# A hybrid attention block on one core: the hyperbolic stage as one stream of 32 heads, with ScalarE on four chunks per instruction

## What is computed

```python
q_h, k_h, v_h = exp_map(x @ W_q.T), exp_map(x @ W_k.T), exp_map(x @ W_v.T)    # per head, 16 wide
arg    = max(1 + 2*c*|q - k|^2 / max((1 - c|q|^2) * (1 - c|k|^2), EPS), 1 + EPS)
dist   = arccosh(arg) / sqrt(c)
w      = softmax(-beta * dist - attention_bias)
out    = log_map(exp_map(w @ log_map(v_h)))                                   # per head
result = concat(out) @ W_o.T
```

## Time and profile before

| | |
|---|---|
| median of 3 runs | 6000.16 us |
| the profiled execution | 6001.92 us |
| its span | 6000.0 us |
| hyperbolic stage in it | about 2370 to 5916 us |
| granted TensorE clock, mean | 0.815 |
| busy: TensorE / VectorE / ScalarE / GpSimd | 67% / 78% / 75% / 24% |

### The profile page before, as it was taken

The page is one execution under the profiler, slowest core; times in us unless marked ns, Lnnn a source line. Parts: engine busy times, 40 slices in busy tenths (PEclk is TensorE's granted clock), DMA queues, the critical chain, the costliest instruction groups (busy, mean ns, idle before and its releaser), DMA issues. The chain is left out here.

```text
span 6000.0 us, 69126 instructions
## 1 busy us (share of the span) xinstructions
PE 4044.0 (67%) x22020; PEld 1836.9 (31%) x22020; DVE 4672.1 (78%) x7192; ACT 4511.1 (75%) x3666; POOL 1445.0 (24%) x1219
## 2 busy tenths in 40 slices
PE   8999999999999998444444444445354444444447
PEld 5555555555555555111110101003111111111104
DVE  7666666766666666788989899984889898989875
ACT  4555555555555553399999999995499999999993
POOL 0000000000000000144444444430244444444430
PEclk9999999999999998677777777777566777777767
DMA  1000000000000001388888888884588888888882
GB/s 38 5 5 5 8 5 6 5 5 5 5 5 5 5 2 34 100 179 180 187 180 187 177 186 177 185 173 114 130 186 182 181 187 180 187 180 187 178 172 74
DMA packets 137266, 628.67 MB, mean 105 GB/s; under 512 B 28102, under 2 KB 66184, under 8 KB 66696
## 3 DMA queue, kind: packets, MB, share of 16 engines
q0 software_dynamic: 73728, 536.90, 44.7%
q1 hardware_dynamic: 63112, 86.55, 4.2%
HBM read 65.30 MB, written 21.23 MB: 14 GB/s over the span
## 5 line engine op out<-in xcount | busy, mean ns | idle before, releaser
L1381 DVE SCALAR_TENSOR_TENSOR b_tiles<-b_ra_rep,b_cap,psum 128x1024 f32<-128x1024 f32 x1024 | 1261.1, 1271 | 247.5 <-PE psum L1620 235.0
L674 DVE CUSTOM_DVE_ANT_0 a_srow<-psum,a_bias 128x512 f32<-128x512 f32 (+3 forms) x1280 | 725.7, 607 | 494.2 <-PE psum L855 491.1
L1620 PE MATMUL psum<-b_qT,b_kT 126*128 126x512 bf16 x2048 | 761.4, 482 | 502.6 <-DVE b_tiles L1381 500.2
L733 ACT ACTIVATE a_pT<-psum 128x512 f32<-128x512 f32 (+3 forms) x1056 | 512.1, 527 | 657.1 <-PE psum L867 656.7
L1633 PE MATMUL psum<-b_tiles,b_v_aug 128*32 128x512 f32 x2464 | 447.3, 810 | 680.4 <-ACT b_tiles L1533 680.3
L867 PE MATMUL psum<-ident,a_srow 128*128 128x128 f32 x4352 | 625.8, 280 | 70.5 <-DVE a_pT L547 32.9
L1388 DVE TENSOR_SCALAR b_tiles<-b_tiles 128x2048 f32<-128x2048 f32 x512 | 665.9, 1301 | 5.5
L751 ACT ACTIVATE a_srow<-a_srow,a_nmax 128x1536 f32<-128x1536 f32 (+15 forms) x512 | 610.5, 1198 | 23.1 <-DVE a_nmax L680 21.2
L855 PE MATMUL psum<-a_k,a_q 64*128 64x512 f32 (+3 forms) x2560 | 623.5, 572 | 0.0
L1633 PE MATMUL psum<-X,b_v_aug 128*32 128x512 f32 x1632 | 295.8, 809 | 443.3 <-ACT X L1533 443.3
L1533 ACT ACTIVATE b_tiles<-b_tiles,b_sc 128x4096 f32<-128x4096 f32 x154 | 585.6, 3802 | 5.1
(11 more groups left out here) (208 smaller groups left out, 5504.4 us busy)
## 6 DMA issues: line engine op xcount, KB each, us to landing
b_tiles<-b_tiles POOLq DMA_DIRECT2D x308, 1024.0 KB, 12.5
X<-b_tiles POOLq DMA_DIRECT2D x204, 1024.0 KB, 13.0
b_ra_rep<-ra_scratch SPq DMA_DIRECT2D x32, 1024.0 KB, 6.7
x_scratch<-X SPq DMA_DIRECT2D x8, 1024.0 KB, 10.5
kv_scratch<-b_tiles SPq DMA_DIRECT2D x4, 2048.0 KB, 8.5
X<-x_scratch SPq DMA_DIRECT2D x8, 1024.0 KB, 9.5
X<-in_x_dram SPq DMA_DIRECT2D x8, 512.0 KB, 6.8
a_wqk<-in_wqk_dram SPq DMA_DIRECT2D x32, 128.0 KB, 2.6
```

The source lines that it names most:

```text
L674: nc.vector.tensor_tensor_reduce(out=srow[:, n % ROWS, h, a:z], in0=bank(c % 2 * 2 + h, 0, z - a), in1=bias[:, h, off + a:off + z], scale= ...
L1381: nc.vector.scalar_tensor_tensor(out=a[:, s * HALF:(s + 1) * HALF], in0=ra_rep[:, j, s * HALF:(s + 1) * HALF], scalar=cap[:, j, k:k + 1], ...
L1620: last = nc.tensor.matmul(half_ps(s)[:, i * BANK:(i + 1) * BANK], kT[:, j, k * P:(k + 1) * P], qT[:, j, cs], start=True, stop=True)
```

## The change

It touches the hyperbolic stage alone, apart from a layer norm semaphore and tiles for the norm statistics of their own.

- Both batches are projected first (32 tiles in one loop). The factors of batch 0 are made in the middle, those of batch 1 at the end. GpSimd scales q, k and v of both batches.
- q, k, v and the factors of all 32 heads go to DRAM (`row_scratch`). One stream of 512 chunks follows, with no break between the batches. Each head's operands are loaded from there, and its output is stored to `o_scratch`.
- One output projection of 32 tiles follows.
- ScalarE's Sqrt, Ln and Exp take four chunks (8192 columns) in one instruction. The y ring has 12 slots, in runs of four; the a ring keeps 7. V_LAG is 12.

```diff
-BATCHED = 4
-SQUARES = "DDPD" * 4
-A_SLOTS = [6, 7, 8, 9, 14, 2, 5]
-Y_SLOTS = [10, 11, 12, 13, 15, 16, 17, 18, 3, 4]
+ROOTS, KEPT = 4, 4
+WIDE = 4
+SQUARES = "DDPD"
+A_SLOTS = [12, 4, 5, 14, 13, 10, 11]
+Y_SLOTS = [0, 1, 2, 3, 6, 7, 8, 9, 15, 16, 17, 18]
 A_BACK, Y_BACK = len(A_SLOTS), len(Y_SLOTS)
 AHEAD = 16
-V_LAG = 10
+V_LAG = 12
...
+            scale(0)
+            pool.wait_ge(S["tok_scaled"], 3)
+            for part in range(3):
+                prepare(pool, nc.gpsimd, 0, part)
+            take_v(pool, nc.gpsimd, 0)
+            for part in range(3):
+                prepare(pool, nc.gpsimd, 1, part)
+            scale(1)
...
+            def root(c):
+                for i in range(c, c + WIDE):
+                    act.wait_ge(S["sq_" + by(i)], squared(i))
+                y = y_slot(c, WIDE)
+                nc.scalar.activation(y, y, ACT.Sqrt, bias=-1.0).then_inc(S["root_done"], 1)
+
+            def weight(c):
+                for i in range(c, c + WIDE):
+                    act.wait_ge(*summed(i))
+                y = y_slot(c, WIDE)
+                nc.scalar.activation(y, y, ACT.Ln).then_inc(S["ln_done"], 1)
+                act.wait_ge(S["ln_done"], pairs_to(c))
+                nc.scalar.activation(y, y, ACT.Exp, bias=col(SHIFT), scale=col(NEG_S)).then_inc(S["w_done"], 1)
```

More of the change, by code:

```diff
@@ new lines, in _, with squares, sums @@
+            scale(0)
[6 more added lines that the diff above has]
+            scale(1)
+            def squares(a, z):
+                for c in range(a, z):
+                    square_by(pool, nc.gpsimd, "P", c)
+            def sums(a, z):
+                for c in range(a, z):
+                    pool.wait_ge(S["root_done"], pairs_to(c))
+                    nc.gpsimd.dma_start(y_slot(c), a_slot(c), accum_op=ALU.add).then_inc(S[f"sum{c % 8}"], 16)
@@ new lines, in _ @@
+            todo = []
+            for g in range(HEADS):
+                if g + 2 < HEADS:
+                    todo += [(g * NCHK + 4 * n + 8, "prepare", g + 2, n) for n in range(3)]
+                if g + 1 < HEADS:
+                    todo += [(g * NCHK + 12, "v", g + 1, 0)]
+            todo.sort(key=lambda e: (e[0], e[1] != "v"))
+            squares(*root_batches[0])
+            for n, (a, z) in enumerate(root_batches):
+                sums(a, z)
+                if n + 1 < len(root_batches):
+                    squares(*root_batches[n + 1])
+                while todo and todo[0][0] <= z:
+                    _, what, g, part = todo.pop(0)
+                    if what == "v":
+                        take_v(pool, nc.gpsimd, g)
+                    else:
+                        prepare(pool, nc.gpsimd, g, part)
@@ L1258, in _ @@
+            assert not todo
+            pool.wait_ge(S["o_ready"], 1)
+            scale_out(nc.gpsimd, 1).then_inc(S["o_scaled1"], 1)
         @block.vector
@@ new lines, in _ @@
+            dve.wait_ge(S["o_loaded0"], 16)
+            out_scale(HEADS - 1)
+            dve.wait_ge(S["o_done"], HEADS * 4)
+            o_scales(0)
+            scale_out(nc.vector, 0).then_inc(S["o_scaled0"], 1)
+            o_factors(1)
+            o_scales(1)
+            dve.sem_inc(S["o_ready"], 1)
+            for t in range(NT):
+                dve.wait_ge(S["out_done"], t + 1)
+                dve.wait_ge(x_back[t * 4 // NT], 16)
+                xt = env.X[:, t, :]
+                nc.vector.tensor_tensor(xt, bank(2 + t % 2, 0, D), xt, ALU.add).then_inc(S["x_added"], 1)
+                dve.wait_ge(S["x_added"], t + 1)
+                after.sums(t)
@@ new lines, in out_transposes @@
+            def out_transposes(g):
+                pe.wait_ge(S["o_copied"], g + 1)
+                pe.wait_ge(S["grp_copied"], min(g + 3, HEADS) * 4)
+                for c in range(4):
+                    last = nc.tensor.transpose(bank(6, c * P, (c + 1) * P), o_sb[:, c * P:(c + 1) * P], env.ident[:, :])
+                last.then_inc(S["oT_done"], 1)
+            for g in range(HEADS):
+                for k in range(NCHK):
+                    c = g * NCHK + k
+                    scores(c)
+                    if c >= V_LAG:
+                        product(c - V_LAG)
+                    if g + 1 < HEADS and 8 <= k < 12:
+                        if k == 8 and g >= 2:
+                            pe.wait_ge(S["o_done"], (g - 1) * 4)
+                        group(g + 1, k - 8)
+                    if g and k == O_AT + 1:
+                        out_transposes(g - 1)
+                if g + 1 < HEADS:
+                    pe.wait_ge(S["grp_copied"], (g + 2) * 4)
@@ new lines, in _ @@
+            transpose_out(0)
+            for t in range(NT):
+                if t + 1 < NT:
+                    transpose_out(t + 1)
+                pe.wait_ge(S["loT_copied"], t + 1)
+                if t >= 2:
+                    pe.wait_ge(S["x_added"], t - 1)
+                for c in range(KC):
+                    last = nc.tensor.matmul(bank(2 + t % 2, 0, D), oT[:, t % 2, c * P:(c + 1) * P], wo_sb[:, c, :],
+                                            start=(c == 0), stop=(c == KC - 1))
+                last.then_inc(S["out_done"], 1)
```

867 lines of the change are left out of this document (426 added, 441 removed).

## The result

The changed kernel takes **6094.58 us** (median of four runs, 6093.38 to 6098.9) against 5999.9 for the kernel before (5994.64 to 6000.69): a ratio of 1.0161, 95% interval 1.0143 to 1.0179, slower by 95 us. The prediction was 6072, 22.6 less, with a range from 5905 to 6150. The profiled execution takes 6093.38 us around a span of 6091.6, at a mean granted clock of 0.797.

The account below looks back on a forecast made before the run. ScalarE set the pace before; afterwards a loop of waits (Sqrt, DMA landing, argument, square, table load) would. Front, 126 periods of 26.0 and the end sum to +72 us on 6000.16: 6072 us, range 5905 to 6150.

Parts of the forecast that it names:

- The period: Hyperbolic stage: a loop from one wide Sqrt to the next takes 26.0 us per four chunks, against 24.55 before.
- the 500 to 600 that was named as a sign: VectorE's idle time before its arguments, waiting for adding DMAs: some 500 to 600 us in the stage.
- Rivals 1 and 3: 1: ScalarE still bounds, period 24.1, 5833 us, chance 0.09; 3: GpSimd or broadcast load adds 96, 6168 us, chance 0.06.
- The wide instructions: ScalarE's four-chunk Sqrt, Ln and Exp: Sqrt takes 7.03 us, and ScalarE alone would have a period of 23.9.
- each head's hiccup: Small disturbance each head brings to ScalarE's stream, raising its own period from 23.9 to 24.1 us.
- The front: Way from projection to the second group's Sqrt: first argument at about 2542, that Sqrt at about 2606; good to 15.
- the wait for slot 10: Sixth argument waits for its slot, free at about 2585 after batch 1's scaling and stores, some 15 us late.
- The stream: From the second group's Sqrt at 2606, 126 periods of 26.0 us lead to the last Sqrt at 5882.
- The last sums: Adding DMAs of the last group land 30.1 us after its Sqrt; then Ln and Exp take 14.3.
- the term put at nothing: DMA: broadcast load of a head's row and the new loads and stores cost nothing, with 4 us in hand.
- The end: From the last Exp to the last statistics, output projection of 32 tiles included: 62 us, ending at 5988.
- rival 4: The skill page's drain: a table load costs 2.66 us, not 1.29; 174 us more, 6246 us, chance 0.01.

Follow-up runs that it names:

- first experiment: Changed kernel with VectorE's square of the chunk before moved ahead of the argument; 5849.51 us, ratio 0.9746 to the kernel before.
- second experiment: Changed kernel with the Sqrt table load issued ahead of the waits for the four squares; 5942.81 us, ratio 0.9895 to the kernel before.
- fourth experiment: Changed kernel with VectorE, not GpSimd, scaling q, k and v of both batches; 6081.01 us, ratio 1.0133 to the kernel before.

## Why the prediction was right, and where it was off

**The period: right, 25.93 against 26.0.** Its steps, forecast first and then the turn shown above: the wide Sqrt 7.03 and 7.03; to the first issue 0.31 and 0.55; to the second landing 12.45 and about 12.2 (3516.74 to just before 3528.99); argument and square 4.66 and 4.67; waking and table load 1.39 and 1.39. The two that missed, 0.24 more and some 0.23 less, cancel; that is luck, if a small one. VectorE's two waits are 3.65 and 0.85, where about 3 and 1.7 were forecast. Where a head's small work stands ahead of a wait it is shorter (0.16 at 3503.10, behind the scaling of a head's output), and the sum over the stage, 450, lies below the 500 to 600 that was named as a sign. The first and second experiments each took one link out, and the period fell as the link's removal should have it, to ScalarE's own 24.0 and to 24.73. Rivals 1 and 3 are out: ScalarE did not bound, and nothing added to the loop.

**The wide instructions: right.** 7.03, 7.03 and 7.22 us, and ScalarE's own period is the 23.94 of the first experiment against 23.9. The surcharge of 0.1 for each head's hiccup turned out as 0.06 in the mean (24.00).

**The front: 21 us short.** The step that failed is the one that put down VectorE's path through the front as its own instructions plus waits. Two instructions of different engines were taken to run beside each other, and they did not.

- The first argument was at 2556.3, not 2542: 14.3 late. At batch 0's scaling VectorE was held for 20.6 us (21.72 less 1.13). This is more than 14.3, so the other terms of that sum came out some 6 too long together.
- Batch 1's scaling took GpSimd 26.22 us, not the 21.6 of the forecast. But the wait for slot 10, put at 15 us, never came: the sixth argument starts at 2601.76 with no idle time ahead of it. VectorE was late by itself, as two clamps and a square had been stretched by 18.5 us. From the first argument to the sixth are 45.4 us, where the forecast had 43: the sum was nearly right here, by luck, for a reason that it did not have.
- From the sixth argument to the second Sqrt are 25.6 us, not 21.3: at the eighth argument VectorE waits 3.53 us for the first adding DMA, so the ring already holds the second group.

14.3, 2.4 and 4.3 make the 21 between 2606 and 2627.3. The fourth experiment shows the cause of both stretched parts: without GpSimd's scaling the instructions have their own lengths, and the way to the first Sqrt is 12.4 us shorter although VectorE then does the scaling itself.

**The stream.** 126 periods of 0.07 less gave 9 us back: the last Sqrt is at 5894.2, 12 after the 5882 of the forecast. That the errors of the front and of the period have opposite signs is luck.

**The last sums: 5 us short.** Ln starts 35.0 after the last Sqrt, not 30.1. The step that failed is the term put at nothing: the new loads and stores were given 4 us in hand under "DMA", but behind the last Sqrt nothing is in hand. The load of batch 0's outputs (`o_scratch`, 2 MB) is still under way when the last four sums are issued at 5901.51. Two rows of the changed kernel, its issue and its time to landing, and the same two of the run with V_LAG 10:

```profile
5896.00 27.41 SPq L1250 DMA_DIRECT2D b_tiles<-o_scratch  x2
...
b_tiles<-o_scratch SPq DMA_DIRECT2D x1, 2048.0 KB, 13.6
...
7182.31 0.32 SPq L1250 DMA_DIRECT2D b_tiles<-o_scratch  x1
...
b_tiles<-o_scratch SPq DMA_DIRECT2D x1, 2048.0 KB, 7.4
```

In the changed kernel the load lands at about 5909.6, and the first of the last sums lands 11.7 us after its issue, where the median of the stage's groups is 7.2. With V_LAG 10 the load has landed at about 7189.7, before the sums are issued at 7192.44; the first lands 7.25 after its issue, and Ln starts 31.3 after the last Sqrt. The other five runs with four chunks per instruction are like the changed kernel (load under way, Ln 35.0 to 35.3 after the last Sqrt). No experiment moved the load by itself, so this is read from the traces.

**The end: right.** 62.2 us from the last Exp to the last statistics, forecast 62 (its four terms make 62.7).

Together: 12.2 at the last Sqrt and 5.3 up to the last Exp, 2.3 behind the stage (the span grew by 91.6, the stage's end by 89.3), and 3.0 because the profiled execution of before lay 1.8 above its median and that of the changed kernel 1.2 below. This is the 22.6 between forecast and measurement, up to roundings.

**The page's drain.** Rows of the changed kernel show 1.28 for a load, 1.29 to the next instruction and 0.02 ahead of it, now behind instructions of 8192 columns too, so rival 4 is out. The Trainium skill (ScalarE: Activation LUTs, What ACT_TABLE_LOAD costs) puts a drain of 1.38 us on top; the period without any waits, 23.94, leaves no room for it (two loads of 1.28 and three instructions of 7.03, 7.03 and 7.22 make 23.84).

## What to carry to other kernels

When an instruction is made wider, write down when each of its inputs is needed and each of its results comes: a Sqrt of four chunks wants its last square 4.8 us sooner and starts its DMAs 3.4 us later, and this turned a free wait on a ring into the bound, though each instruction got cheaper. Then order the queue of the engine in the middle so that what the wide instruction waits for stands ahead of whatever waits for its results: this cost nothing and moved the time by 245 us. Judge a change of two parts by its parts: here one was worth 101 us less and the other 196 more, and mended it was worth 55 less. And before the rows of two profiled runs are set side by side, look where a block that no edit touches ends in each: in the runs here the last statistics ahead of the stage end between 2362.1 and 2373.9 us, and a shift of 6 us there hid that the fourth experiment's edit makes the first argument 6 us later.

## What the runs showed of the hardware that was not expected

GpSimd's tensor_tensor of 128x4096 between two tensors in SBUF (7.17 us each) and VectorE's f32 instructions on SBUF exclude each other for a whole instruction: 8.19 for a clamp of 1.22, 6.87 for a square of 2.28, 21.72 for three normalizations of 1.13, and 26.22 instead of 21.52 for GpSimd's three where it was held in turn. VectorE's argument, with PSUM among its inputs, ran at its 2.46 in the middle of it. In the changed kernel's stream GpSimd's squares of some 3.6 us do little harm: none of them lies beside one of VectorE's clamps or squares, only beside arguments, copies out of PSUM and waits (VectorE's 508 clamps there have a mean of 1.26 us). In the first experiment some do, and its clamps have a mean of 1.34. The Trainium skill (SBUF — State Buffer, SBUF: two separate sides) has the rule: the pair of ports that VectorE and GpSimd share is an exclusive lock, held for a whole instruction, and VectorE needs it in a mode that uses two ports or with two inputs in SBUF. The trace agrees, with the numbers above. The clamp's row names one input, so of the page's two cases the mode is left for it; no run here shows the mode by itself.
